# A graph attention layer on one core: the source one-hot is compared with node numbers kept in PSUM, and the score lives in PSUM

## Chip, cores and metric

The kernel runs on one core of a Trainium2 chip. The metric is the device time of one execution in microseconds, the median over several runs; lower is better.

## What is computed

A graph of 6250 nodes with 64 features each and 206250 edges, sorted by destination. Edge features go through a linear layer, source and destination nodes through three, and each node sums the weighted messages of its edges:

```python
Qh = (x @ Wq.T + bq).reshape(n, H, D)          # H = 4 heads, D = 16
Kh = (x @ Wk.T + bk).reshape(n, H, D)
Vh = (x @ Wv.T + bv).reshape(n, H, D)
Ee = (edge_attr @ We.T + be).reshape(-1, H, D)
score = (Kh[src] * Qh[dst] * (1.0 / np.sqrt(D)) * Ee).sum(-1)
score = jnp.exp(jnp.clip(score, -5.0, 5.0))
msg = Vh[src] * score[..., None]
wV = jax.ops.segment_sum(msg, dst, num_segments=n)
out = layernorm(x + wV.reshape(n, H * D))
```

## The kernel before

It has three stages. The first (to about 53 us) computes the tables of K and V (kv_table) and of Q (q_table) in HBM and makes the constants. The middle stage (to about 1797 us) goes once over the edges. The last adds x and normalises.

The middle stage works on 202 groups of 8 tiles of 128 edges (the last group has 4 tiles), with four slots of buffers, so that slot = group mod 4. Each engine has its own instruction stream, the same for every group but for the slot's parity, and semaphores with running counts order them. There is no planner: the order on each engine is that of its `step` function.

K and V of an edge's source node come in two ways. Most tiles are fetched by GpSimd, one indirect DMA of 128 rows per tile (L258, "gather"): 6 tiles in a group of even number, 7 in one of odd number. The other tiles, 2 and 1, are fetched by TensorE, for groups 2 to 199, with a one-hot: the 6250 nodes are cut in V = 7 blocks of 896 nodes, and a node's place in its block is p * U + u, with p the partition and U = 7 values of u. VectorE makes src_onehot (L784) with 128 x 896 elements, by comparing r_row (each edge's place in its block, a row spread over all partitions) with node_of (the numbers p * U + u, each repeated 128 times). TensorE multiplies it with x, split in two parts x_hi and x_lo, 14 matmuls of 448 columns into one of two xg_banks (L652, L653, `gather_x`). Of the 7 blocks VectorE keeps the right one (L795 x_sel and L801 xg_sb, `select_x`), and TensorE transposes it (L663) and projects it to K and V (L670), which ACT copies to kv (L756).

A step of VectorE for group g: kq = K times Q (L820, waits for the gathers and for L756), the sums of group g - 1 added to acc (L810, `add_sums`), kqe (L826), score (L829, a sum over D), score_c (L833, the clip), then for an even g a src_onehot of group g + 2 and for an odd g a select_x of group g + 1, then msg (L840, waits for ACT's exponential, L746, into p_ps), select_x of group g + 2, and src_onehot of group g + 3. Three src_onehot are made for two groups.

A step of TensorE for group g: the edges' linear layer of g + 1 (L615, L618), Q of g + 1 (L631), gather_x for g + 2, transposes for g + 1, the sums of messages of g (L641, waits for msg), the projection for g + 1, and for an even g a second gather_x for g + 2.

GpSimd issues the gathers of group g once its indices are loaded and msg of group g - 4 has been made, so it may run up to four groups ahead. SyncE loads all else.

PSUM has eight banks of 128 x 512 words. The two xg_banks are used in columns 0 to 447 of 512. Bank sum_ps holds two sums of messages (in 64 partitions), p_ps in columns 256 to 287, and is free beyond. src_onehot, r_row and node_of lie in SBUF, and so do score and score_c.

Of the kernel before, what the change touches and what calls it, by code (L numbers as in the profile page):

```python
# [5 lines left out]
F32 = mybir.dt.float32  # L6
F32R = mybir.dt.float32r
BF16 = mybir.dt.bfloat16
I32 = mybir.dt.int32
ALU = mybir.AluOpType  # L10
# [4 lines left out]
P = 128  # L15
N = 6250
E = 206250
F = 64
H = 4
# [5 lines left out]
T = 8  # L25
# [15 lines left out]
U = 7  # L41
V = 7
# [14 lines left out]
def gnn_kernel(nc, xT, x_blocks, w_kvq, We_t, be_row, src_tab, src_rows, src_cols, dst_tab,  # L57
               dst_rows, dst_first, attr, out):
    ctx = ExitStack()
    with ctx:  # L60
        def sb(name, shape, dt, stack=ctx):
            return stack.enter_context(nc.sbuf_tensor(name, shape, dt))

        def ps(name, shape, dt):
            return ctx.enter_context(nc.psum_tensor(name, shape, dt))

        def sem(name):
            return ctx.enter_context(nc.semaphore(name))
# [11 lines left out]
        src_block = sb("src_block", [P, Q], F32)  # L80
        minus_row = sb("minus_row", [P, G], F32)
        iota_v = sb("iota_v", [P, F * V], F32)
        node_of = sb("node_of", [P, U, P], F32)
        xg_t_sb = sb("xg_t_sb", [P, 2, P], F32)
        dst_neg = sb("dst_neg", [P, G, T], F32)
        base_i = sb("base_i", [P, G], I32)
# [14 lines left out]
        first = ExitStack()  # L101
# [16 lines left out]
        one_pass = sb("one_pass", [P, 1], F32, first)  # L118
        iota_i = sb("iota_i", [P, W], I32, first)
        iota_v_i = sb("iota_v_i", [P, F * V], I32, first)  # L120
        node_of_i = sb("node_of_i", [P, U, P], I32, first)
        row_i = sb("row_i", [P, 1], I32, first)
        row_f = sb("row_f", [P, 1], F32, first)
        x_nat = sb("x_nat", [P, U, F * V], F32, first)
# [9 lines left out]
        xg_banks = [ps(f"xg_bank{i}", [P, 4, P], F32) for i in range(2)]  # L134
        turn_bank = ps("turn_bank", [P, 4, P], F32)
        sum_ps = ps("sum_ps", [P, 4, P], F32)
        p_ps = sum_ps[:, 2, 0:T * H]
        kv_banks = [ee_ps[0], ee_ps[1], qe_ps[0], qe_ps[1]]
        q_banks = [turn_bank, sum_ps, xg_banks[0]]

# [19 lines left out]
        constants_made = sem("constants_made")  # L160
# [8 lines left out]
        iota_set = sem("iota_set")  # L169
# [52 lines left out]
        src_onehot_made = sem("src_onehot_made")  # L222
# [22 lines left out]
        def first_q(i, j):  # L245

            return (i + j // SLOTS) * PE_EACH + PE_BEFORE[j % SLOTS] - PE_SKIPPED
# [7 lines left out]
        def gather(pool, g, slot, first=0, end=T):  # L255

            for t in range(first, min(end, pool_tiles(g, slot))):
                pool.indirect_dma_start(  # L258
                    out=kv[:, slot, t, :], out_offset=None, in_=kv_table,
                    in_offset=bass.IndirectOffsetOnAxis(ap=idx[:, slot, t:t + 1], axis=0))\  # L260
                    .then_inc(kv_gathered[slot], 16)


        with nc.Block() as block:
# [37 lines left out]
            @block.gpsimd  # L302
            def _(pool):
                for c in range(DVE_ONES, CHUNKS):
                    pool.memset(xT_sb[F:P, c * CH * P:(c + 1) * CH * P], 1.0).then_inc(ones_set[1], 1)

                pool.wait_ge(ones_set[1], CHUNKS - DVE_ONES)
                pool.memset(we_sb[:, :], 0.0).then_inc(consts_zeroed, 1)
                pool.memset(be_sb[:, :, :], 0.0).then_inc(consts_zeroed, 1)
                pool.memset(q_win[:, :, :, :, :], 0.0).then_inc(consts_zeroed, 1)  # L310
                pool.memset(ones[:, :], 1.0).then_inc(consts_zeroed, 1)
                pool.memset(ident[:, :], 0.0).then_inc(ident_zeroed, 1)
                pool.wait_ge(ident_zeroed, 1)
                pool.affine_select(out=ident[:, :], in_=ident[:, :], compare_op=ALU.not_equal, fill=1.0,
                                   base=0, pattern=[[-1, P]], channel_multiplier=1).then_inc(ident_set, 1)
                pool.memset(xg_t_sb[:, :, :], 1.0).then_inc(consts_zeroed, 1)
                pool.iota(iota_i[:, :], pattern=[[1, W]], base=0, channel_multiplier=0).then_inc(iota_set, 1)
                pool.iota(iota_v_i[:, :], pattern=[[0, F], [1, V]], base=0, channel_multiplier=0).then_inc(iota_set, 1)
                pool.iota(node_of_i[:, :, :], pattern=[[1, U], [0, P]], base=0, channel_multiplier=U).then_inc(iota_set, 1)
                pool.wait_ge(iota_set, 3)  # L320
                pool.iota(row_i[0:W, :], pattern=[[0, 1]], base=0, channel_multiplier=1).then_inc(iota_set, 1)
                pool.iota(row_i[W:2 * W, :], pattern=[[0, 1]], base=0, channel_multiplier=1).then_inc(iota_set, 1)
                pool.wait_ge(iota_set, 5)

                pool.wait_ge(be_loaded, 16)
                pool.tensor_copy(be_parts[:, 0, :], be_f[:, :]).then_inc(be_step, 1)
                pool.wait_ge(be_step, 1)
                pool.tensor_tensor(be_rest[:, :], be_f[:, :], be_parts[:, 0, :], ALU.subtract).then_inc(be_step, 1)
                pool.wait_ge(be_step, 2)
                pool.tensor_copy(be_parts[:, 1, :], be_rest[:, :]).then_inc(be_step, 1)  # L330
                pool.wait_ge(be_step, 3)
                pool.tensor_tensor(be_parts[:, 2, :], be_rest[:, :], be_parts[:, 1, :], ALU.subtract).then_inc(be_step, 1)
                pool.wait_ge(be_step, 4)
                for part in range(3):
                    row = slice(32 * part, 32 * part + 1)
                    pool.tensor_copy(be_sb[row, :, :], be_parts[row, part:part + 1, :].to_broadcast([1, T, F]))\
                        .then_inc(be_step, 1)
                    pool.wait_ge(be_step, 5 + part)
                pool.wait_ge(idx_first, 16 * SLOTS)
                pool.wait_ge(kv_stored, 16 * CHUNKS)  # L340
                gather(pool, 0, 0, 0, EARLY[0])
                pool.wait_ge(limits_set, 4)
                pool.partition_all_reduce(limits_all[:, :], limits[:, :], P,
                                          bass.bass_isa.ReduceOp.max).then_inc(limits_joined, 1)
                for g in range(1, len(EARLY)):
                    gather(pool, g, g, 0, EARLY[g])
# [61 lines left out]
            def _(dve):  # L408
# [38 lines left out]
                check_destinations(5)  # L447
                dve.wait_ge(iota_set, 5)
                dve.tensor_copy(iota_w[:, :], iota_i[:, :]).then_inc(dst_step, 1)
                dve.tensor_copy(node_of[:, :, :], node_of_i[:, :, :]).then_inc(constants_made, 1)  # L450
                dve.tensor_copy(row_f[:, :], row_i[:, :]).then_inc(constants_made, 1)

                dve.wait_ge(src_loaded, 32)
# [14 lines left out]
                def third_part(c):  # L468
                    dve.wait_ge(q_part1, c + 1)
                    dve.tensor_tensor(q_stage[:, c * CH:(c + 1) * CH, 2, :], q_rest[:, c % 2, :, :],  # L470
                                      q_stage[:, c * CH:(c + 1) * CH, 1, :], ALU.subtract).then_inc(q_staged, 1)

                for c in range(CHUNKS):
# [6 lines left out]
                    if c >= 1:  # L480
                        third_part(c - 1)
                third_part(CHUNKS - 1)

                dve.wait_ge(x_split[0], 1)
                dve.tensor_tensor(x_lo[:, :, :], x_nat[:, :, :], x_hi[:, :, :], ALU.subtract).then_inc(x_split[1], 1)
                dve.wait_ge(limits_joined, 1)
# [12 lines left out]
                dve.tensor_scalar(base_i[:, :], base_f[:, :], one_pass[:, :], None, ALU.mult).then_inc(dst_step, 1)  # L499
                dve.scalar_tensor_tensor(out=dst_neg[:, :, :], in0=base_b, scalar=minus_general[:, :],  # L500
                                         in1=dst_neg[:, :, :], op0=ALU.mult, op1=ALU.add).then_inc(dst_step, 1)
                dve.wait_ge(constants_made, 3)
                dve.wait_ge(dst_step, 9)
                dve.tensor_scalar(minus_row[:, :], base_i[:, :], -1.0, row_f[:, :], ALU.mult, ALU.subtract)\
                   .then_inc(dst_step, 1)
# [8 lines left out]
        middle = ExitStack()  # L514
# [9 lines left out]
        xg_sb = sb("xg_sb", [P, 2, 2, F], F32, middle)  # L524
        kq = sb("kq", [P, T, F], F32, middle)
        kqe = sb("kqe", [P, T, F], F32, middle)
        score = sb("score", [P, T * H], F32, middle)
        score_c = sb("score_c", [P, T * H], F32, middle)
        msg = sb("msg", [P, 2, T, F], F32, middle)

        with nc.Fori(0, passes) as this_pass:
            with nc.Block() as block:
# [242 lines left out]
                def _(dve):  # L775
                    def make_src_onehot(g, i, j, k):

                        q, slot = first_q(i, j) + k, j % SLOTS
                        parity = (PE_BEFORE[slot] - PE_SKIPPED + k) % 2
                        if k == 0:  # L780
                            dve.wait_ge(r_loaded[slot], 16 * (i + j // SLOTS + (1 if slot >= PE_FROM else 0)))
                        if not (isinstance(q, int) and q < 2):
                            dve.wait_ge(x_gathered, q - 1)
                        dve.tensor_tensor(src_onehot[:, parity, :, :],  # L784
                                          r_row[:, slot, k:k + 1, :].to_broadcast([P, U, P]),
                                          node_of[:, :, :], ALU.is_equal).then_inc(src_onehot_made, 1)

                    def select_x(g, i, j, k):

# [23 lines left out]
                    def step(g, i, j):  # L813
# [21 lines left out]
                        if pe_tiles(g + 2, (j + 2) % SLOTS) == 2:  # L835
                            make_src_onehot(g + 2, i, j + 2, 1)
# [10 lines left out]
                        if pe_tiles(g + 3, (j + 3) % SLOTS):  # L847
                            make_src_onehot(g + 3, i, j + 3, 0)

                    make_src_onehot(PE_FROM, 0, PE_FROM, 0)  # L850
                    for g in range(SLOTS):
                        step(g, 0, g)
# [180 lines left out]
```

## Time and profile before

| | |
|---|---|
| median of 3 runs | 1816.32 us (1814.88 to 1819.0) |
| span of the profiled execution, first to last instruction | 1816.0 us |
| TensorE matmul busy | 1671.1 us (92%) |
| TensorE weight load busy (beside matmul) | 1483.1 us (82%) |
| VectorE busy | 1320.3 us (73%) |
| ScalarE (ACT) busy | 968.4 us (53%) |
| GpSimd busy | 1366.6 us (75%) |
| mean granted TensorE clock | 0.976 |

The profiled execution's time is known by its span; the runs' times stand at most 3 us from it. Busy time of an engine leaves out its waits and also the time in which it issues; engines work side by side, so the shares add up to more than one. L12 is line 12 of the kernel; PE is TensorE, PEld its weight load, DVE is VectorE, ACT is ScalarE, POOL is GpSimd. Idle time is given with what ended it; "issue" is idle time in which nothing is seen that was waited for.

### The profile page before, as it was taken

Reading aid. Unit: us, or ns where it says so; the run is one execution under the profiler, and the core shown is the slowest. Engines: PE = TensorE matmul, PEld = TensorE weight load, DVE = VectorE, ACT = ScalarE, POOL = GpSimd, SP = SyncE. Lnnn points to the kernel's source line nnn. Section 1 sums busy time; section 2 is a strip of 40 time slices with the busy share of each in tenths; the row PEclk is TensorE's granted clock in tenths of the full one; section 3 lists DMA queues with packets and bytes.
Section 4 is the critical chain, followed back from the end, with each engine's and each line's share of the span. In section 5 each row is a group of like instructions: output and inputs, shape, how many; then the busy total and the mean of one; then the engine's idle time right before and its main releaser. Section 6 shows DMA issues by size and latency. Waiting matters only on the chain. (4 is left out here: it accounts for less than half of the span.)

```text
span 1816.0 us, 47296 instructions
## 1 busy us (share of the span) xinstructions
PE 1671.1 (92%) x13047; PEld 1483.1 (82%) x13047; DVE 1320.3 (73%) x2197; ACT 968.4 (53%) x2864; POOL 1366.6 (75%) x1348
## 2 busy tenths in 40 slices
PE   6399999999999999999999999999999999999994
PEld 6388888888888888888888888888888888888883
DVE  6377777777777777777777777777777777777774
ACT  5355555555555555555555555555555555555553
POOL 5677777777777777777777777777777777777774
PEclk8699999999999999999999999999999999999995
DMA  7455444444444444444444444444444444444441
GB/s 234 129 139 136 127 132 126 127 126 129 130 123 124 134 129 124 128 133 127 128 133 127 122 132 130 125 125 135 127 124 125 133 129 125 123 128 132 127 114 61
DMA packets 198830, 234.44 MB, mean 129 GB/s; under 512 B 96742, under 2 KB 123180, under 8 KB 198684
## 3 DMA queue, kind: packets, MB, share of 16 engines
q1 hardware_dynamic: 156732, 147.96, 27.7%
q0 software_dynamic: 42080, 86.26, 19.5%
q8 instruction: 8, 0.13, 0.0%
q14 instruction: 10, 0.08, 0.0%
HBM read 226.67 MB, written 7.38 MB: 129 GB/s over the span
## 5 line engine op out<-in xcount | busy, mean ns | idle before, releaser
L258 POOL DMA_INDIRECT kv<-kv_table,idx x1315 | 1348.7, 1026 | 416.4 <-issue 402.2
L652 PE MATMUL xg_bank<-x_hi,src_onehot 128*128 128x448 f32 x2079 | 786.5, 378 | 6.7 <-DVE src_onehot L784 6.7
L653 PE MATMUL xg_bank<-x_lo,src_onehot 128*128 128x448 f32 x2079 | 759.7, 365 | 0.0
L723 ACT ACTIVATE distance<-iota_w,dst_neg 128x64 f32<-128x64 f32 x1612 | 428.4, 339 | 0.0
L652 PEld LDWEIGHTS xg_bank<-x_hi,src_onehot 128*128 128x128 f32 x2079 | 391.8, 188 | 35.3 <-DVE src_onehot L784 6.9
L653 PEld LDWEIGHTS xg_bank<-x_lo,src_onehot 128*128 128x128 f32 x2079 | 392.3, 189 | 27.3
L820 DVE TENSOR_TENSOR kq<-kv,qe_ps 128x512 f32<-128x512 f32 x202 | 138.5, 686 | 332.3 <-DMA kv<-kv_table,idx 325.6
L784 DVE TENSOR_TENSOR src_onehot<-r_row,node_of 128x896 fp32r<-128x896 f32 x297 | 322.9, 1087 | 25.0 <-DMA r_row<-r_table 25.0
L641 PE MATMUL sum_ps<-onehot,msg 128*64 128x64 f32 x3224 | 228.4, 225 | 77.6 <-DVE msg L840 77.6
L641 PEld LDWEIGHTS sum_ps<-onehot,msg 128*64 128x64 f32 x3224 | 208.8, 139 | 102.9 <-DVE msg L840 100.9
L749 ACT COPY xg_t_sb<-turn_bank 64x256 f32<-64x256 f32 x198 | 61.9, 312 | 330.6 <-PE turn_bank L663 240.8
L795 DVE SCALAR_TENSOR_TENSOR x_sel<-iota_v,src_block,xg_bank 128x448 f32<-128x448 f32 x297 | 201.1, 677 | 44.0 <-PE xg_bank L653 36.3
L618 PEld LDWEIGHTS ee_ps<-we_sb,attr_sb 128*128 128x128 f32 x1612 | 215.0, 194 | 6.5
L618 PE MATMUL ee_ps<-we_sb,attr_sb 128*128 128x128 f32 x1612 | 214.7, 277 | 0.0
L746 ACT ACTIVATE sum_ps<-score_c 128x32 f32<-128x32 f32 x202 | 40.5, 201 | 317.8 <-DVE score_c L833 317.7
L801 DVE TENSOR_REDUCE xg_sb<-x_sel 128x64 f32<-128x448 f32 x297 | 184.2, 620 | 10.2
L631 PE MATMUL qe_ps<-q_win,onehot_t 128*128 128x128 bf16 x2418 | 169.5, 220 | 2.2 <-DMA q_win<-q_table 1.6
L631 PEld LDWEIGHTS qe_ps<-q_win,onehot_t 128*128 128x128 bf16 x2418 | 153.7, 99 | 5.1 <-DMA q_win<-q_table 2.7
L709 ACT ACTIVATE dst_square<-dst_row,minus_row 128x512 f32<-128x512 int32 x202 | 143.6, 711 | 20.1 <-DMA dst_row<-dst_rows 20.1
L829 DVE TENSOR_REDUCE score<-kqe 128x32 f32<-128x512 f32 x202 | 138.3, 685 | 6.9
L840 DVE TENSOR_TENSOR msg<-kv,sum_ps 128x512 f32<-128x512 f32 x202 | 136.7, 677 | 1.1 <-ACT sum_ps L746 1.1
L826 DVE TENSOR_TENSOR kqe<-kq,ee_ps 128x512 f32<-128x512 f32 x202 | 136.3, 675 | 1.1 <-issue 0.3
(116 smaller groups left out, 1049.4 us busy)
## 6 DMA issues: line engine op xcount, KB each, us to landing
attr_sb<-attr SPq DMA_DIRECT2D x201, 256.0 KB
dst_row<-dst_rows SPq DMA_DIRECT2D x402, 128.0 KB
kv<-kv_table,idx POOLq DMA_INDIRECT x1315
r_row<-r_table SPq DMA_DIRECT2D x99, 128.0 KB, 3.1
q_win<-q_table SPq DMA_DIRECT2D x404, 24.0 KB
r_row<-r_table SPq DMA_DIRECT2D x99, 64.0 KB, 2.9
idx<-src_tab SPq DMA_DIRECT2D x206, 4.0 KB, 4.1
kv_table<-kv_stage SPq DMA_DIRECT2D x7, 448.0 KB, 3.8
```

What stands on the lines that cost most here:

```text
L258: pool.indirect_dma_start(out=kv[:, slot, t, :], out_offset=None, in_=kv_table, in_offset=bass.IndirectOffsetOnAxis(ap=idx[:, slot, t:t + ...
L618: mm = pe.matmul(ee[:, k * P:(k + 1) * P], attr_sb[:, slot, k * P:(k + 1) * P], we_sb[:, :], start=False, stop=(k == n - 1))
L631: mm = pe.matmul(bank(qe_ps[slot % 2], n * P)[:, k * P:(k + 1) * P], onehot_t[:, slot % 2, k * P:(k + 1) * P], q_win[:, slot, :, s, :], st ...
L641: mm = pe.matmul(sum_ps[0:F, slot % 2, 0:W], msg[:, slot % 2, t, :], onehot[:, slot, t, :], start=(t == 0), stop=(t == n - 1))
L652: pe.matmul(xg, src_onehot[:, parity, u, :], x_hi[:, u, :], start=(u == 0), stop=False)
L653: mm = pe.matmul(xg, src_onehot[:, parity, u, :], x_lo[:, u, :], start=False, stop=(u == U - 1))
L709: act.activation(dst_square[:, 0:n], dst_row[:, slot, 0:n], ACT.Square, bias=minus_row[:, ds(g, 1)]).then_inc(dst_squared, 1)
L723: made = act.activation(distance[:, t, :], iota_w[:, :], ACT.Square, bias=dst_neg[:, ds(g, 1), t:t + 1].rearrange("p o t -> p (o t)"))
L784: dve.tensor_tensor(src_onehot[:, parity, :, :], r_row[:, slot, k:k + 1, :].to_broadcast([P, U, P]), node_of[:, :, :], ALU.is_equal).then_ ...
L795: dve.scalar_tensor_tensor(out=x_sel[:, :, :].rearrange("p f v -> p (f v)"), in0=iota_v[:, :], scalar=src_block[:, ds(q, 1)], in1=bank(xg_ ...
L801: dve.tensor_reduce(xg_sb[:, j % 2, k, :], x_sel[:, :, :], AX_X, ALU.add).then_inc(x_summed, 1)
L820: dve.tensor_tensor(kq[:, 0:n, :], kv[:, slot, 0:n, 0:F], qe_ps[slot % 2][:, 0:n, :], ALU.mult).then_inc(kq_made, 1)
```

## The change

node_of is no longer a table of 128 x 896 words in SBUF. Its seven numbers for each partition are copied into columns 448 to 454 of both xg_banks, and L784 reads those of the bank of its parity, each number 128 times by a step of zero. The iota that makes them has 7 columns instead of 896. The cast in the setup goes, and two copies of seven columns are made later in the setup, after the last use of xg_banks[0] for Q. score and score_c move to columns 288 to 319 and 320 to 351 of bank sum_ps, so that L829 writes PSUM, L833 reads and writes it, and L746 reads it. No wait in the loop changes.

```diff
-        node_of = sb("node_of", [P, U, P], F32)
...
-        node_of_i = sb("node_of_i", [P, U, P], I32, first)
+        node_of_i = sb("node_of_i", [P, U], I32, first)
...
         p_ps = sum_ps[:, 2, 0:T * H]
+        score = sum_ps[:, 2, T * H:2 * T * H]
+        score_c = sum_ps[:, 2, 2 * T * H:3 * T * H]
+        node_of = [b[:, 3, F * V - 3 * P:F * V - 3 * P + U] for b in xg_banks]
...
-                pool.iota(node_of_i[:, :, :], pattern=[[1, U], [0, P]], base=0, channel_multiplier=U).then_inc(iota_set, 1)
+                pool.iota(node_of_i[:, :], pattern=[[1, U]], base=0, channel_multiplier=U).then_inc(iota_set, 1)
...
-                dve.tensor_copy(node_of[:, :, :], node_of_i[:, :, :]).then_inc(constants_made, 1)
...
+                for parity in range(2):
+                    dve.tensor_copy(node_of[parity], node_of_i[:, :]).then_inc(constants_made, 1)
+
                 dve.wait_ge(x_split[0], 1)
...
-                dve.wait_ge(constants_made, 3)
+                dve.wait_ge(constants_made, 4)
...
-        score = sb("score", [P, T * H], F32, middle)
-        score_c = sb("score_c", [P, T * H], F32, middle)
...
                         dve.tensor_tensor(src_onehot[:, parity, :, :],
                                           r_row[:, slot, k:k + 1, :].to_broadcast([P, U, P]),
-                                          node_of[:, :, :], ALU.is_equal).then_inc(src_onehot_made, 1)
+                                          node_of[parity].unsqueeze(2).to_broadcast([P, U, P]),
+                                          ALU.is_equal).then_inc(src_onehot_made, 1)
```

## Rows read from the trace of the kernel before

**Rows 1.** Part 1 of the page: busy time, share of the span, instructions.
```profile
PE 1671.1 (92%) x13047; PEld 1483.1 (82%) x13047; DVE 1320.3 (73%) x2197; ACT 968.4 (53%) x2864; POOL 1366.6 (75%) x1348
```

**Rows 2.** Groups by line: busy us, mean ns | idle us before, and its releasers.
```profile
L258 POOL DMA_INDIRECT kv<-kv_table,idx x1315 | 1348.7, 1026 | 416.4 <-issue 402.2 <-DVE msg L840 8.2 <-DMA kv_table<-kv_stage 6.0
...
L784 DVE TENSOR_TENSOR src_onehot<-r_row,node_of 128x896 fp32r<-128x896 f32 x297 | 322.9, 1087 | 25.0 <-DMA r_row<-r_table 25.0
...
L795 DVE SCALAR_TENSOR_TENSOR x_sel<-iota_v,src_block,xg_bank 128x448 f32<-128x448 f32 x297 | 201.1, 677 | 44.0 <-PE xg_bank L653 36.3
...
L801 DVE TENSOR_REDUCE xg_sb<-x_sel 128x64 f32<-128x448 f32 x297 | 184.2, 620 | 10.2
...
L820 DVE TENSOR_TENSOR kq<-kv,qe_ps 128x512 f32<-128x512 f32 x202 | 138.5, 686 | 332.3 <-DMA kv<-kv_table,idx 325.6 <-ACT kv L756 3.6 <-PE qe_ps L631 2.8
...
L840 DVE TENSOR_TENSOR msg<-kv,sum_ps 128x512 f32<-128x512 f32 x202 | 136.7, 677 | 1.1 <-ACT sum_ps L746 1.1
...
L833 DVE TENSOR_SCALAR score_c<-score 128x32 f32<-128x32 f32 x202 | 38.0, 188 | 7.0
```

**Rows 3.** GpSimd in order of time, the end of the gathers: start, duration in us.
```profile
1771.01 0.94 POOL L258 DMA_INDIRECT kv<-kv_table,idx  x1 [0.30 <-issue]
...
1789.74 0.94 POOL L258 DMA_INDIRECT kv<-kv_table,idx  x1 [0.30 <-issue]
```

**Rows 4.** Busy time of each engine in two stretches, clock, DMA share.
```profile
core 0: us, PE busy (x) PEld busy (x) DVE busy (x) ACT busy (x) POOL busy (x), PEclk, DMA share, GB/s
200.00:330.00 130.00, 130.00 (x1032) 116.26 (x1031) 100.80 (x166) 74.58 (x226) 100.42 (x98) 1.00 0.48 127
340.00:1790.00 1450.00, 1364.16 (x10684) 1205.12 (x10682) 1063.62 (x1757) 777.99 (x2345) 1116.26 (x1096) 0.99 0.47 127
```

**Rows 5.** GpSimd and VectorE in order of time: stretched gathers and one L784.
```profile
100.81 1.43 POOL L258 DMA_INDIRECT kv<-kv_table,idx  x1 [0.30 <-issue]
...
903.04 1.08 DVE L784 TENSOR_TENSOR src_onehot<-r_row,node_of 128x896 fp32r<-128x896 f32 x1
903.24 1.70 POOL L258 DMA_INDIRECT kv<-kv_table,idx  x1 [0.30 <-issue]
...
1756.93 1.29 POOL L258 DMA_INDIRECT kv<-kv_table,idx  x1 [0.30 <-issue]
```

**Rows 6.** What VectorE waited for, 200 to 330 us: total us, times, longest.
```profile
DVE x_sel L795 <- PE xg_bank L653: 18.6, 8, 2.5
DVE kq L820 <- DMA kv<-kv_table,idx: 3.1, 2, 2.4
```

**Rows 7.** VectorE in order of time: kq of groups 4, 24, 40 and 190.
```profile
111.01 0.69 DVE L820 TENSOR_TENSOR kq<-kv,qe_ps 128x512 f32<-128x512 f32 x1 [0.33 <-ACT kv L756]
...
272.39 0.69 DVE L820 TENSOR_TENSOR kq<-kv,qe_ps 128x512 f32<-128x512 f32 x1 [0.21 <-ACT kv L756]
...
405.89 0.69 DVE L820 TENSOR_TENSOR kq<-kv,qe_ps 128x512 f32<-128x512 f32 x1 [1.05 <-DMA kv<-kv_table,idx]
...
1699.68 0.69 DVE L820 TENSOR_TENSOR kq<-kv,qe_ps 128x512 f32<-128x512 f32 x1 [1.13 <-DMA kv<-kv_table,idx]
```

**Rows 8.** GpSimd in order of time: first and last gather of group 4.
```profile
83.47 0.94 POOL L258 DMA_INDIRECT kv<-kv_table,idx  x1 [6.38 <-DVE msg L840]
...
90.63 0.94 POOL L258 DMA_INDIRECT kv<-kv_table,idx  x1 [0.31 <-issue]
```

**Rows 9.** VectorE in order of time: kq of groups 199 to 201, one msg.
```profile
1777.18 0.69 DVE L820 TENSOR_TENSOR kq<-kv,qe_ps 128x512 f32<-128x512 f32 x1 [5.10 <-DMA kv<-kv_table,idx]
...
1780.01 0.69 DVE L840 TENSOR_TENSOR msg<-kv,sum_ps 128x512 f32<-128x512 f32 x1 [0.27 <-ACT sum_ps L746]
1787.16 0.69 DVE L820 TENSOR_TENSOR kq<-kv,qe_ps 128x512 f32<-128x512 f32 x1 [6.46 <-DMA kv<-kv_table,idx]
...
1792.78 0.42 DVE L820 TENSOR_TENSOR kq<-kv,qe_ps 128x256 f32<-128x256 f32 x1 [1.84 <-DMA kv<-kv_table,idx]
```

**Rows 10.** VectorE in order of time: setup, the wait ahead of x_lo.
```profile
46.10 3.42 DVE L485 TENSOR_TENSOR x_lo<-x_nat,x_hi 128x3136 fp32r<-128x3136 f32 x1 [2.08 <-ACT x_hi L403]
```

## The prediction

> **What bounds the kernel now.** I read the page first. TensorE is busy for 92% of the span and GpSimd for 75% [rows 1], which points at TensorE. But the GpSimd row counts only the bodies of the gathers: the group of L258 has 1315 gathers of 1026 ns on the mean, and the idle time before them is 402.2 us of "issue", that is of nothing that it waited for. On the other side stands VectorE, whose kq of each group sat idle for 325.6 us in all until gathered rows had landed [rows 2]. So GpSimd issues without a stop, and the others wait for what it fetches.
>
> The next view is GpSimd's order of time. Left alone, a gather takes 0.94 us and the next starts 1.2487 us after it: 15 steps from 1771.01 to 1789.74 [rows 3]. That beat is shorter than the 1.326 us of the middle of the run (98 gathers in 130 us, [rows 4]). The difference is stretched gathers, and they have one companion. At 903.24 a gather starts 0.20 us after the source one-hot of L784 began, and takes 1.70 us: 0.76 more, and it ends 0.82 us after L784's end at 904.12, as if most of it only began then [rows 5]. I went through all 1265 gathers that start between 100 and 1780 us. 223 last longer than 0.97 us (the first at 100.81, the last at 1756.93, [rows 5]), and every one of the 223 starts while an L784 is running; no other gather is stretched. Their excess over 0.942 us sums to 101.1 us. L784 is the only instruction in the loop that reads two large tiles from SBUF. 432 gathers began during L820, L826, L840 or L795, which read one tile from SBUF and the other from PSUM, and none was stretched; nor were those begun during the reductions, which read one.
>
> The last view is a comparison of two stretches. Over 200 to 330 us TensorE is busy 130.00 of 130.00 us, and VectorE waits for gathered rows only 3.1 us; over 340 to 1790 us TensorE has 85.8 us idle of 1450 [rows 4, 6]. The first is bound by TensorE, the second by the gathers. Their paces can be read from kq: group 4 at 111.01 and group 24 at 272.39 make 16.14 us for two groups; group 40 at 405.89 and group 190 at 1699.68 make 17.25 [rows 7]. Two groups need 13 gathers (6 and 7, since TensorE fetches 2 and 1 of the tiles), and 17.25 / 13 is 1.327: the stretched beat again. The kernel begins in the first regime because GpSimd has a lead there: the last gather of group 4 starts at 90.63 and kq of group 4 at 111.01 [rows 7, 8]. The lead shrinks by 1.1 us in two groups and is used up near 310 to 335 us.
>
> **The change part by part.** *L784 compares with PSUM.* It keeps its 297 runs and 896 columns, but only r_row comes from SBUF. By the 432 unstretched gathers it then holds up no gather. GpSimd's path from group 4 on: its first gather starts at 83.47 (held by msg of group 0, which doesn't change), its last at 1789.74 [rows 3, 8]. That is 1285 steps in 1706.27 us; at 1.2487 each they are 1604.6, so 101.7 us less, which agrees with the 101.1 summed above. What follows the last gather is fixed: kq of group 201 starts at 1792.78 [rows 9] and the span ends at 1816.0. By this path alone the span is 1816.0 - 101.7 = 1714.3.
>
> Here a rule of the Trainium skill speaks against the change. The row is the 1.70 us gather above [rows 5]. The page "SBUF — State Buffer", section "Who interferes with whom", says that GpSimd blocks against a VectorE instruction with two SBUF inputs only where it reads SBUF itself, and infers that a tensor_tensor leaves the generation of DMA descriptors alone, since that needs only the write side. By that inference there would be nothing to win and the sum would be 0 instead of 101.7. The trace disagrees for these gathers, which also read their indices from SBUF; the same section's first half fits it.
>
> *L784's own time.* Rows of equal width differ by source only a little: 128x448 takes 620 ns as the reduction L801 from SBUF and 677 as L795, which reads a PSUM bank; L840 reads its second input from PSUM with a step of zero, as the new L784 does, and takes 677 for 512 columns against 686 of L820 [rows 2]. So the bounds for L784 are its 1087 ns and 57 more. I take 1087. The upper bound is 0.17 us for two groups (3 one-hots), beside which VectorE has 29.2 us idle in 130, or 3.6 us for two groups, even in the stretch at TensorE's pace [rows 4]. That idle time hides it; without that cover it would cost 101 x 0.17 = 17 us.
>
> *TensorE's path.* This is what is late next. The gathers' new beat is 13 x 1.2487 = 16.23 us for two groups, and TensorE's pace 16.14. GpSimd starts with its lead of 111.01 - 91.57 = 19.4 us, of which some 2 are landing time, and now loses only 0.09 us in two groups, 9 us in the whole loop. So the lead never runs out, and TensorE sets the pace almost to the end. Group 198 is 97 pairs after group 4: its kq starts at 111.01 + 97 x 16.14 = 1676.6. Groups 198 to 201 have nothing left for TensorE to fetch but one tile of 199, and a step there is short: in the tail kq to the end of msg is 3.5 us (1777.18 to 1780.70, [rows 9]), and with the sums, the projection and its copy about 4.5. That puts kq of 199, 200 and 201 at 1681, 1685 and 1689 by the engines' own work. GpSimd, which still has 7, 8 and 4 gathers to do, allows them at 1777.18, 1787.16 and 1792.78 less 101.7: 1675.5, 1685.5 and 1691.1 [rows 9]. The gathers come last by about 2 us, and the end stays at 1714.3. So the two limits nearly meet, and nothing beyond the stretch is won.
>
> *Bank order.* The new L784 reads the bank that TensorE fills for the same parity. Its wait for x_gathered and TensorE's wait for src_onehot_made were there before; no wait is added. The same holds for score and score_c in the bank of the sums: VectorE writes score only after add_sums, which has waited for sums_made.
>
> *Score and clip in PSUM.* No row shows VectorE writing PSUM. L829 and L833 keep their widths, and L833 has 188 ns [rows 2]; by the 57 ns that at most separated a read of PSUM from one of SBUF, I bound the two together at nothing and 0.1 us more, and take nothing. They are under the idle time named above, and only the four tail groups would show it, 0.4 us. No gather is stretched by L833 alone, so nothing is won there.
>
> *Setup.* The cast of 128x896 goes; it can't have cost more than L784 at the same width, 1.1 us. Two copies of 7 columns come, each about as long as L833 (0.19 us, [rows 2]), placed ahead of L485, where VectorE idles 2.08 us for ACT's x_hi [rows 10]: they go into that wait, and cost 0.4 us without it. The smaller iota lies on GpSimd ahead of the 6.0 us for which its first gather waits for kv_table [rows 2]. Bounds: from 1.1 us won to 0.4 lost; I take 0.
>
> **Sum.** 1816.0 - 101.7 = 1714.3 for the span. A run's time stands 0.3 us above it (median 1816.32), and GpSimd, now closer behind msg in the first groups, may wait there up to 1 us more. Forecast: 1715 us, 5.6% faster. Its own range is 1707 to 1722.
>
> **Rivals.** *TensorE takes over at a worse pace.* For it: the slack at the end is only 2 us, 16.14 was read over ten pairs, and with longer one-hots or with TensorE never idle the pace might slip. Against it: the 130 us without idle time at a granted clock of 1.00, the 2.4 GHz level [rows 4]. Each 0.1 us in two groups adds 9.7 us once the 2 are gone; at 16.3 the time is 1714 + 16 - 2, about 1728.
>
> *Nothing changes,* as it would if the hold came from what L784 writes, or from its reading r_row, and not from the pair of inputs (the inference of the Trainium skill's page cited above would give the same time). Against it: L795 and L840 also read SBUF and write SBUF, without one stretched gather. Time 1816. A partial hold would lie between.
>
> *Slower: reading seven numbers 128 times each from PSUM is slow.* If L784 took twice its time, 2.17 us, VectorE's own chain for two groups would go from about 14.2 (2 x 3.5 of kq to msg with gaps, 3 x 2.4 of one-hot, select and reduce) to 17.5, above both 17.25 and 16.14: 85 pairs at 0.25 and 13 at 1.4 more, some 39 us, 1855. It decides from about 1 us more for one instruction. Against it is the 677 ns of L840, whose second input is just such a read.
>
> **Chances.** Forecast 0.78; TensorE at a worse pace (1722 to 1745) 0.12; nothing or a part (above 1745, to 1816) 0.06, 0.03 of it without a change; slower 0.03; faster than 1707 0.01. From 1707 to 1740 I leave out about 0.13. A difference under 0.2% (3.6 us) can't be told from none. Faster: 0.94; within 0.2%: 0.03; slower: 0.03.
>
> **What the profile after would show.** L258's mean falls from 1026 to about 946 ns, with no gather over 0.97 us in the loop. L784 stays near 1087 ns. kq's wait for gathered rows shrinks from 325.6 us to under 30, mostly in the last groups, and x_sel's wait for TensorE (18.6 us in the early 130 us, [rows 6]) grows to over 150. kq goes at 16.14 us for two groups from start to end, and TensorE's busy share is 97% or more. The prediction is wrong if stretched gathers remain (the hold isn't the pair of inputs), if L784 is well above 1.14 us, or if TensorE's pace exceeds 16.2.

## The result and the profile after

The changed kernel takes 1715.97 us (median of 4 runs, 1715.64 to 1717.27) against 1815.88 for the kernel before beside it: a ratio of 0.9453, interval 0.9436 to 0.9471, which is 5.5% faster. The profiled execution's span is 1713.8 us.

The page of the changed kernel answers to [rows 1]:

```profile
PE 1649.7 (96%) x13047; PEld 1479.4 (86%) x13047; DVE 1318.6 (77%) x2198; ACT 960.6 (56%) x2864; POOL 1263.1 (74%) x1348
```

GpSimd lost 103 us of busy time; VectorE kept its own within 2 us and ACT within 8. TensorE's fell by 21 us for the same 13047 instructions: its records are 10 us shorter in sum and overlap by 11 us more, and no work went from it. Work shrank only for the gathers. The groups by line answer to [rows 2]:

```profile
L260 POOL DMA_INDIRECT kv<-kv_table,idx x1315 | 1246.1, 948 | 416.5 <-issue 388.1
...
L798 DVE SCALAR_TENSOR_TENSOR x_sel<-iota_v,src_block,xg_bank 128x448 f32<-128x448 f32 x297 | 202.0, 680 | 248.5 <-PE xg_bank L655 240.7
L786 DVE TENSOR_TENSOR src_onehot<-r_row,xg_bank 128x896 fp32r<-128x896 f32 x297 | 320.0, 1078 | 24.8 <-DMA r_row<-r_table 24.8
...
L823 DVE TENSOR_TENSOR kq<-kv,qe_ps 128x512 f32<-128x512 f32 x202 | 137.9, 683 | 28.5 <-ACT kv L758 23.5
```

The mean gather went from 1026 to 948 ns. kq no longer waits for gathered rows (325.6 us before), and VectorE's waiting has moved to x_sel, which waits for TensorE. That is how a change of bound looks: the same idle time, with another releaser. In order of time, GpSimd and then VectorE near the place of [rows 5]:

```profile
905.73 0.94 POOL L260 DMA_INDIRECT kv<-kv_table,idx  x1 [0.30 <-DVE msg L843]
906.98 0.94 POOL L260 DMA_INDIRECT kv<-kv_table,idx  x1 [0.30 <-issue]
908.23 0.95 POOL L260 DMA_INDIRECT kv<-kv_table,idx  x1 [0.31 <-issue]
```

```profile
906.83 1.08 DVE L786 TENSOR_TENSOR src_onehot<-r_row,xg_bank 128x896 fp32r<-128x896 f32 x1
```

The gather of 906.98 begins 0.15 us into a one-hot and takes 0.94 us; before, one that began at 0.20 took 1.70. Of all gathers from 100 us to the end, 253 began during an L786, and none of them, and none of the others, is longer than 0.97 us. Before, 252 gathers had begun during an L784 (100 to 1780 us), and 223 of them were stretched. The windows answer to [rows 4], and three kq, of groups 4, 40 and 190, to [rows 7]:

```profile
200.00:330.00 130.00, 130.00 (x1035) 116.43 (x1034) 102.65 (x171) 73.98 (x226) 98.17 (x104) 1.00 0.51 136
340.00:1690.00 1350.00, 1343.58 (x10684) 1202.31 (x10683) 1062.05 (x1756) 770.23 (x2344) 1019.35 (x1080) 1.00 0.51 135
```

```profile
110.24 0.69 DVE L823 TENSOR_TENSOR kq<-kv,qe_ps 128x512 f32<-128x512 f32 x1 [0.33 <-ACT kv L758]
...
400.81 0.69 DVE L823 TENSOR_TENSOR kq<-kv,qe_ps 128x512 f32<-128x512 f32 x1 [0.22 <-ACT kv L758]
...
1611.83 0.69 DVE L823 TENSOR_TENSOR kq<-kv,qe_ps 128x512 f32<-128x512 f32 x1 [0.29 <-ACT kv L758]
```

TensorE is busy for 99.5% of the long stretch (340 to 1690 us), where it was for 94% (340 to 1790), and the 150 groups from 40 to 190 go at 16.15 us for two, the pace that the kernel before had only in its first 300 us. The kernel ends with the rows that answer to [rows 9], kq of groups 199 to 201:

```profile
1682.19 0.69 DVE L823 TENSOR_TENSOR kq<-kv,qe_ps 128x512 f32<-128x512 f32 x1 [2.01 <-ACT kv L758]
...
1685.64 0.68 DVE L823 TENSOR_TENSOR kq<-kv,qe_ps 128x512 f32<-128x512 f32 x1
...
1690.42 0.42 DVE L823 TENSOR_TENSOR kq<-kv,qe_ps 128x256 f32<-128x256 f32 x1 [0.37 <-DMA kv<-kv_table,idx]
```

### The profile page after: what moved, and what is told of

Read it like the earlier page. It is cut to its first block and busy times, and to the rows that moved or that the text cites. A ratio compares the mean times of both kernels' runs of the same rounds, so it can differ in the third digit from the quotient of the medians.

```text
span 1713.8 us, 47297 instructions
## 1 busy us (share of the span) xinstructions
PE 1649.7 (96%) x13047; PEld 1479.4 (86%) x13047; DVE 1318.6 (77%) x2198; ACT 960.6 (56%) x2864; POOL 1263.1 (74%) x1348
## 5 line engine op out<-in xcount | busy, mean ns | idle before, releaser
L260 POOL DMA_INDIRECT kv<-kv_table,idx x1315 | 1246.1, 948 | 416.5 <-issue 388.1
L798 DVE SCALAR_TENSOR_TENSOR x_sel<-iota_v,src_block,xg_bank 128x448 f32<-128x448 f32 x297 | 202.0, 680 | 248.5 <-PE xg_bank L655 240.7
L786 DVE TENSOR_TENSOR src_onehot<-r_row,xg_bank 128x896 fp32r<-128x896 f32 x297 | 320.0, 1078 | 24.8 <-DMA r_row<-r_table 24.8
L643 PE MATMUL sum_ps<-onehot,msg 128*64 128x64 f32 x3224 | 224.4, 223 | 8.6 <-DVE msg L843 8.6
L832 DVE TENSOR_REDUCE sum_ps<-kqe 128x32 f32<-128x512 f32 x202 | 140.0, 693 | 6.9
L829 DVE TENSOR_TENSOR kqe<-kq,ee_ps 128x512 f32<-128x512 f32 x202 | 135.4, 670 | 0.3 <-issue 0.3
L736 ACT ACTIVATE onehot<-distance 128x512 f32<-128x512 f32 x202 | 127.5, 631 | 10.4
```

Source lines behind the costliest of these rows:

```text
L260: pool.indirect_dma_start(out=kv[:, slot, t, :], out_offset=None, in_=kv_table, in_offset=bass.IndirectOffsetOnAxis(ap=idx[:, slot, t:t + ...
L643: mm = pe.matmul(sum_ps[0:F, slot % 2, 0:W], msg[:, slot % 2, t, :], onehot[:, slot, t, :], start=(t == 0), stop=(t == n - 1))
L786: dve.tensor_tensor(src_onehot[:, parity, :, :], r_row[:, slot, k:k + 1, :].to_broadcast([P, U, P]), node_of[parity].unsqueeze(2).to_broad ...
L798: dve.scalar_tensor_tensor(out=x_sel[:, :, :].rearrange("p f v -> p (f v)"), in0=iota_v[:, :], scalar=src_block[:, ds(q, 1)], in1=bank(xg_ ...
L832: dve.tensor_reduce(score[:, 0:n * H], kqe[:, 0:n, :].rearrange("p t (h d) -> p (t h) d", d=D), AX_X, ALU.add).then_inc(score_summed, 1)
```

## Experiments

Two things were open: what in the old one-hot held the gathers, and whether the new time really is one where two limits meet. The runs fell on chips in two conditions. On the first two chips the kernel before itself took 2749.65 and 2664.51 us instead of 1816. It has no trace there, but in the traces of the kernels beside it TensorE issued with gaps. A piece of the weight loads, in order of time, from the kernel of the first experiment:

```profile
1035.34 0.19 PEld L654 LDWEIGHTS xg_bank<-x_hi,src_onehot 128*128 128x128 f32 x1 [0.55 <-issue]
1036.07 0.19 PEld L655 LDWEIGHTS xg_bank<-x_lo,src_onehot 128*128 128x128 f32 x1 [0.55 <-issue]
1036.79 0.19 PEld L654 LDWEIGHTS xg_bank<-x_hi,src_onehot 128*128 128x128 f32 x1 [0.53 <-issue]
1037.51 0.28 PEld L655 LDWEIGHTS xg_bank<-x_lo,src_onehot 128*128 128x128 f32 x1 [0.54 <-issue]
1038.92 0.29 PEld L654 LDWEIGHTS xg_bank<-x_hi,src_onehot 128*128 128x128 f32 x1 [1.13 <-issue]
```

One load each 0.72 us or twice that, where 0.20 is usual, and nothing that it waits for. From 100 us on this kernel has 777 steps between weight loads of more than 0.6 us, 965 us in all; the changed kernel on the chip of the result has none. On such a chip the length of the gathers can still be read, but the time says nothing of them, because GpSimd isn't the bound. So each run is read for what its chip can show.

**One half of the change at a time.** The first kernel takes the one-hot's part alone:

```diff
-        score = sum_ps[:, 2, T * H:2 * T * H]
-        score_c = sum_ps[:, 2, 2 * T * H:3 * T * H]
...
+        score = sb("score", [P, T * H], F32, middle)
+        score_c = sb("score_c", [P, T * H], F32, middle)
```

> The source one-hot compares with PSUM as in the change, score and score_c stay in SBUF. Main theory (only the one-hot held GpSimd's gathers): the time of the changed kernel, 1716 us, no gather over 0.97 us. Rival (the fp32 clip from SBUF to SBUF holds gathers too): some of the 101 us comes back, stretched gathers begin during the clip; each could cost at most its 0.19 us, 202 x 0.19 = 38 us, so up to 1754.

> The one-hot alone in PSUM, score and score_c in SBUF, once more. Main theory: no stretched gather (mean 948 ns); where TensorE issues without gaps 1716 us against 1816 us of the kernel before, where it has gaps (the kernel before at 2660 to 2750 us) the same time as the kernel before within 1.5%, because GpSimd then waits for msg and not for itself. Rival (score in PSUM carries a part of the 100 us): above 1720 us where TensorE has no gaps.

The second takes the score's part alone (the same lines the other way round, in the kernel before):

> Only score and score_c in PSUM, the one-hot compares with the SBUF table as before. Main theory: 1816 us, within 3 us, some 220 stretched gathers with 101 us of excess. Rival (the clip holds gathers): up to 38 us faster.

Where TensorE had gaps: one-hot alone 2757.59 us, ratio 1.0061 (1.0019 to 1.0103), mean gather 949 ns; score alone 2750.52 us, ratio 0.9974 (0.9926 to 1.0023), mean gather 989 ns. Groups by line, of the one and of the other:

```profile
L258 POOL DMA_INDIRECT kv<-kv_table,idx x1315 | 1247.7, 949 | 1441.9 <-DVE msg L843 1060.3 <-issue 376.1 <-DMA kv_table<-kv_stage 5.5
```

```profile
L260 POOL DMA_INDIRECT kv<-kv_table,idx x1315 | 1300.3, 989 | 1375.4 <-DVE msg L840 986.4 <-issue 382.2 <-DMA kv_table<-kv_stage 6.8
```

With the score alone the hold is there (40 ns x 1315 = 53 us of GpSimd's time: 172 stretched gathers, every one begun during the one-hot, so the rival that the clip holds gathers falls). It is worth nothing here, since GpSimd waits some 1000 us for msg anyway. The 0.6% by which the one-hot alone came out slower has no explanation here. On a chip without gaps the one-hot alone took 1717.55 us, ratio 0.9459 (0.9438 to 0.9481), with a mean gather of 950 ns. The two intervals, this one and that of the whole change, overlap nearly fully: the one-hot's part carries the gain, and the score's part carries none of it that can be seen. The score's part was not timed alone on a chip without gaps.

**Small source, still in SBUF.** It separates PSUM from the size of the table.

```diff
+        node_small = sb("node_small", [P, 2, U], F32)
...
-        node_of = [b[:, 3, F * V - 3 * P:F * V - 3 * P + U] for b in xg_banks]
+        node_of = [node_small[:, b, :] for b in range(2)]
```

> As the changed kernel, but the seven numbers lie in SBUF and are read from there with a step of zero. Main theory (two SBUF inputs hold GpSimd, whatever their size): 1816 us, some 220 stretched gathers. Rival (the hold comes from streaming a table of 896 words, a small or repeated source is harmless): 1716 us.

> The same kernel as the one with the seven numbers in SBUF, on another chip if TensorE issues there without gaps. In the first run on a chip where TensorE has gaps of 0.5 us and more between its instructions, the gathers were stretched again (989 ns on the mean against 949), and the time was that of the kernel before there. Main theory on a chip like the first: 1816 us and a mean of 1026 ns. Rival (a small source is harmless for the time): 1716 us.

Both chips had gaps: 2759.71 us, ratio 1.0039 (0.9994 to 1.0083), and 2680.07 us, ratio 1.001 (0.9966 to 1.0054). The mean gather was 989 and 991 ns; the group of the second:

```profile
L261 POOL DMA_INDIRECT kv<-kv_table,idx x1315 | 1303.2, 991 | 1323.7 <-DVE msg L844 932.5 <-issue 385.6 <-DMA kv_table<-kv_stage 5.7
```

Seven numbers in SBUF hold the gathers as the table did (989 in the run with the table on the same chip as the first). One one-hot of the second run and the gather that began 0.09 us into it:

```profile
293.93 1.08 DVE L787 TENSOR_TENSOR src_onehot<-r_row,node_small 128x896 fp32r<-128x896 f32 x1
294.02 1.80 POOL L261 DMA_INDIRECT kv<-kv_table,idx  x1 [0.30 <-issue]
```

The rival, that a small source is harmless, falls. What it would do to the time where GpSimd is the bound was not measured.

**Inputs swapped.** In every harmless instruction of the trace before, SBUF was the first input.

```diff
-                                          r_row[:, slot, k:k + 1, :].to_broadcast([P, U, P]),
                                           node_of[parity].unsqueeze(2).to_broadcast([P, U, P]),
+                                          r_row[:, slot, k:k + 1, :].to_broadcast([P, U, P]),
```

> As the changed kernel, with the two inputs of the comparison swapped: the PSUM numbers are the first input, the SBUF row the second. In every instruction that left gathers alone in the trace before, the SBUF tile was the first input. Main theory (it takes two SBUF inputs): 1716 us, no stretched gather. Rival (whatever is the second input and lies in SBUF holds GpSimd): about 1816 us and some 220 stretched gathers.

> The kernel with swapped inputs again. It had no stretched gather on the chip with the gaps (949 ns). Main theory on a chip like the first: 1716 us. Rival (the SBUF row as second input holds GpSimd): 1816 us.

Again gaps on both chips: 2747.11 us, ratio 0.9918 (0.9863 to 0.9972), and 2729.06 us, ratio 1.0148 (1.003 to 1.0266). The two contradict each other in sign, which shows how far such a chip's times can be trusted: not within 1.5%. The gathers are clear, 949 and 948 ns; the group of the second run:

```profile
L260 POOL DMA_INDIRECT kv<-kv_table,idx x1315 | 1246.1, 948 | 1409.1 <-DVE msg L843 1012.5 <-issue 389.4 <-DMA kv_table<-kv_stage 7.2
```

So it isn't the place of the SBUF input but that there are two of them.

**Part of the columns.** The comparison is split: 512 columns against SBUF, 384 against PSUM.

```diff
-                        dve.tensor_tensor(src_onehot[:, parity, :, :],
-                                          r_row[:, slot, k:k + 1, :].to_broadcast([P, U, P]),
-                                          node_of[parity].unsqueeze(2).to_broadcast([P, U, P]),
+                        dve.tensor_tensor(src_onehot[:, parity, 0:4, :],
+                                          r_row[:, slot, k:k + 1, :].to_broadcast([P, 4, P]),
+                                          node_small[:, 0:4].unsqueeze(2).to_broadcast([P, 4, P]),
+                                          ALU.is_equal)
+                        dve.tensor_tensor(src_onehot[:, parity, 4:U, :],
+                                          r_row[:, slot, k:k + 1, :].to_broadcast([P, U - 4, P]),
+                                          node_of[parity][:, 4:U].unsqueeze(2).to_broadcast([P, U - 4, P]),
                                           ALU.is_equal).then_inc(src_onehot_made, 1)
```

> The comparison in two instructions: the first 512 of 896 columns against numbers in SBUF, the other 384 against PSUM. Main theory (a gather is held until the reads of the instruction with two SBUF inputs end): the excess goes with the square of the instruction's length, since both the chance of a gather beginning in it and the mean rest of it shrink; (0.59/0.99) squared is 0.36, so 36 us of 101 come back, 1752 us. Rival (the cost goes with the columns): 4/7 of 101, 1774 us. Rival (any such instruction costs a fixed hold): 1816 us.

> The comparison in two instructions: 512 of 896 columns against numbers in SBUF, the other 384 against PSUM. The run on a chip with gaps had a mean gather of 957 ns, against 989 with all 896 columns in SBUF and 948 with none. Main theory (a gather is held until the reads of the instruction with two SBUF inputs end, so the excess goes with about the square of its length): 36 of 101 us come back, some 1752 us, mean gather 975 ns. Rival (the cost goes with the columns): 58 us, 1774 us. Rival (a fixed hold): 1816 us.

With gaps 2724.86 us, without an interval, and a mean gather of 957 ns (65 stretched gathers, 11.3 us). Without gaps 1727.37 us, ratio 0.9512 (0.9494 to 0.953): some 10 us above the changed kernel and below all three expectations. Three groups of the second run say why:

```profile
L261 POOL DMA_INDIRECT kv<-kv_table,idx x1315 | 1254.5, 954 | 416.5 <-issue 399.7 <-DVE msg L849 11.4 <-DMA kv_table<-kv_stage 5.5
...
L788 DVE TENSOR_TENSOR src_onehot<-r_row,node_small 128x512 fp32r<-128x512 f32 x297 | 204.2, 687 | 25.1 <-DMA r_row<-r_table 25.1
...
L829 DVE TENSOR_TENSOR kq<-kv,qe_ps 128x512 f32<-128x512 f32 x202 | 138.0, 683 | 20.0 <-ACT kv L760 12.6 <-issue 1.6
```

The mean gather is 954 ns, not 975. From 100 us on only 14 gathers are stretched, by 4.5 us in all, where the square law gave 36. The hold itself is as that law has it. A gather and its one-hot:

```profile
906.45 0.68 DVE L788 TENSOR_TENSOR src_onehot<-r_row,node_small 128x512 fp32r<-128x512 f32 x1
906.49 1.46 POOL L261 DMA_INDIRECT kv<-kv_table,idx  x1 [0.30 <-issue]
```

The gather ends 0.82 us after the one-hot does, as the one of 903.24 did in the kernel before. So do all the others: the six traces with stretched gathers have 808 of them, and each ends 0.81 to 0.84 us after the end of the instruction with two SBUF inputs in which it began. A gather that is left alone takes 0.94, so it seems that about its first 0.125 us run freely and the rest waits (an estimate: 0.942 less the 0.817 that most of the 808 need afterwards). It loses what is left of that instruction less 0.125 us, and next to nothing if it begins in its last 0.16 us.

What failed is how often they met. The law takes every offset of a gather in the one-hot as equally likely. For the kernel before that comes out at 292 x (1.087 - 0.125)^2 / (2 x 1.2487) = 108 us, where 101 were measured, and for this one at 37. Here two groups take 16.26 us and 13 gathers at this run's beat of 1.251 take 16.26 as well, so the offsets hardly move from one pair of groups to the next: of the 120 gathers that began during an L788, 90 did so in its last 0.16 us. The 14 hits come in four bunches, at 110 to 117, 549 to 572, 906 to 913 and 1297 to 1320 us. That the loss is so small is luck.

The 10 us are not the hold but TensorE's pace. No kq waits for gathered rows, and the last one starts at 1701.66, 6 us after the last gather's start at 1695.69, so that the 4.5 us of hold stay hidden. (1623.23 - 403.73) / 75 is 16.26 us for two groups from kq 40 to kq 190, 0.11 more than in the changed kernel, and 97 times 0.11 is 11 us:

```profile
403.73 0.69 DVE L829 TENSOR_TENSOR kq<-kv,qe_ps 128x512 f32<-128x512 f32 x1
...
1623.23 0.69 DVE L829 TENSOR_TENSOR kq<-kv,qe_ps 128x512 f32<-128x512 f32 x1 [0.15 <-ACT kv L760]
```

From start to start, the weight loads of the source fetch (L656, L657) take 0.07 us more of these 0.11 and those of the transposes 0.04. Why stays open; that 13 gathers also make 16.26 may be chance or a coupling. The times of all three theories in the expectation fell.

**Less work for TensorE.**

```diff
-                            pe.matmul(xg, src_onehot[:, parity, u, :], x_hi[:, u, :], start=(u == 0), stop=False)
-                            mm = pe.matmul(xg, src_onehot[:, parity, u, :], x_lo[:, u, :], start=False, stop=(u == U - 1))
+                            mm = pe.matmul(xg, src_onehot[:, parity, u, :], x_hi[:, u, :], start=(u == 0), stop=(u == U - 1))
```

> The changed kernel without the 7 of 14 matmuls of each source fetch that multiply with x_lo, so that x is fetched with less precision; TensorE loses 3 x 7 x 0.2 = 4.3 us of its 16.14 for two groups. Main theory (GpSimd's path of 1286 gathers at 1.2487 us ends with the kernel too, at most 2 us apart): 1714 us, the changed kernel's time within 4 us, and kq waits for gathered rows again for over 300 us. Rival (TensorE alone is the bound after the change): clearly faster, 100 x 4.3 us less down to VectorE's 14.2 us for two groups, some 1530 us.

> The changed kernel without the 7 of 14 matmuls of each source fetch that multiply with x_lo (x is fetched with less precision), so TensorE loses 3 x 7 x 0.2 = 4.3 us of its 16.14 for two groups. On a chip where TensorE issues without gaps. Main theory (GpSimd's path of 1285 steps of 1.2487 us ends within 2 us of TensorE's): 1714 us, no more than 4 us from the changed kernel, kq waiting for gathered rows again for over 200 us, at 16.23 us for two groups. Rival (TensorE alone is the bound after the change): some 1530 us.

With gaps 2631.3 us, ratio 0.984 (0.9767 to 0.9913): even there 2079 fewer matmuls bought little. Without gaps 1718.27 us, ratio 0.9464 (0.9446 to 0.9482). TensorE's busy time fell from 1649.7 to 1352.6 us and the kernel's time not at all: it is 2 us longer, as its gathers' beat of 1.2510 makes GpSimd's path 3 us longer than at 1.2487. The group of kq and one window:

```profile
L822 DVE TENSOR_TENSOR kq<-kv,qe_ps 128x512 f32<-128x512 f32 x202 | 138.7, 687 | 271.0 <-DMA kv<-kv_table,idx 246.2 <-ACT kv L757 18.3 <-PE qe_ps L633 5.7
```

```profile
340.00:1690.00 1350.00, 1084.72 (x8669) 940.76 (x8833) 1044.03 (x1733) 758.04 (x2314) 1020.72 (x1080) 0.92 0.51 134
```

kq waits for gathered rows again, 246.2 us, and none of the gathers is stretched: this is GpSimd's bare path. It runs from 82.61 to 1690.10, 1285 steps of 1.2510 us. Only in the first groups, where GpSimd still has its lead, does the rest show its own pace: kq of group 4 at 105.52 and of group 14 at 173.92 make 13.7 us for two groups, against 16.25 afterwards.

**Less work for GpSimd.** This kernel leaves out K and V of the first tile of each group, which are zeros there:

```diff
-            for t in range(first, min(end, pool_tiles(g, slot))):
+            for t in range(max(first, 1), min(end, pool_tiles(g, slot))):
```

(and the counts of `gathered` one lower for each group, with kv's first tiles set to zero once).

> The changed kernel without the first gather of every group (that tile's K and V are zeros, set once), so GpSimd has 11 instead of 13 gathers for two groups, 13.7 us. Main theory (TensorE's pace of 16.14 us for two groups sets the loop, GpSimd ends only some 2 us behind it): 1710 to 1716 us, kq still at 16.14 us for two groups, GpSimd waiting for msg for over 200 us. Rival (GpSimd still is the bound after the change and TensorE follows): 202 x 1.25 = 250 us less, down to VectorE's 14.2 us for two groups, some 1530 us.

1713.19 us, ratio 0.9432 (0.9415 to 0.9449), on the same chip as the last. What GpSimd waited for, in the whole span:

```profile
POOL kv L260 <- DVE msg L844: 303.5, 195, 8.0
POOL kv L260 <- issue: 285.5, 917, 4.2
```

202 gathers fewer are 252 us of GpSimd's time. It spends them waiting for msg, 303.5 us, and the kernel gains no more than 3 us (the intervals overlap), 5 against the kernel with less TensorE work. kq goes at (1611.31 - 400.01) / 75 = 16.15. Taken together: without 18% of TensorE's busy time the kernel takes 1718 us, without 15% of the gathers 1713, and with everything 1716. Neither engine alone can be relieved for more than some 3 us. Both relieved together were not run; the 13.7 us for two groups above hint at what the next limit would allow.

## Why the prediction was right

*What bounded the kernel.* Right: 101.6 us less on GpSimd's path gave 100 us less time, with TensorE's work unchanged, and the idle time moved from one releaser to the other. TensorE at 92% was not the bound, and GpSimd at 75% was.

*The hold.* The step "101.7 us less on GpSimd's path" is the whole of the sum. The path from group 4's first gather to the last is now 82.71 to 1687.38, 1604.7 us for the 1604.6 forecast. Its cause, two SBUF inputs in one VectorE instruction, was an inference from some 430 harmless gathers beside instructions that all had SBUF first. The runs with seven numbers in SBUF and with swapped inputs turned it into something shown. The rival that what L784 writes, or r_row, makes the hold fell with the result itself. The page "SBUF — State Buffer" of the Trainium skill, section "Who interferes with whom", infers that a tensor_tensor leaves descriptor generation alone. For these gathers it would have meant no stretch, and 223 were stretched. They also read their indices from SBUF, and that GpSimd is held where it reads SBUF itself fits; whether this read or the making of the descriptors is what waits, no run separates.

*L784's own time.* 1078 ns for 1087 forecast. The small loss of being delayed itself is gone: up to 1164 ns before, for one-hots that began within 0.05 us of a gather's start, and 1087 at most after. Seven numbers read 128 times each from PSUM cost nothing, and the slower rival falls.

*TensorE's path.* 16.15 us for two groups from 40 to 190 (16.14 forecast), group 198's kq at 1676.28 (1676.6), and the last three at 1682.19, 1685.64 and 1690.42 (1681, 1685.5 and 1691.1). The two limits met as worked out, and the last kq still waited 0.37 us for its gathers. That TensorE would take over at a worse pace fell for this kernel; the split comparison shows that such a thing exists and costs 10 us. x_sel's wait for TensorE grew to 240.7 us (over 150 forecast), and kq's for gathered rows fell to 0.4 us (under 30 forecast). TensorE's busy share is 96%, not 97% or more: the forecast took its busy time as unchanged, and it fell by 21 us.

*Score and clip.* L829 went from 685 to 693 ns and L833 from 188 to 199, the exponential from 201 to 181: nothing, as taken.

*Setup.* x_lo (now L489) starts at 45.46 instead of 46.10, after a wait of 1.94 us, and the first gather of group 4 at 82.71 instead of 83.47. The term was taken as 0 inside its bounds; it is about the 0.5 us by which the span came out under 1714.3.

*From span to time.* This small term was read wrongly. Each run's time stands 1.8 to 1.9 us above its own span (1715.64 against 1713.8 for the profiled one), not 0.3: the prediction set the span of one execution against the median of others, which differ by 4 us among themselves. With 1.8 the forecast span of 1714.3 would have given 1716.1. Beside the 100 us neither this nor the 0.5 us above matters.

## What to carry to other kernels

Add a DMA-issuing engine's gaps to its busy time before ruling it out: GpSimd at 75% was full, and the engine at 92% was waiting for it. Where gathers issued by GpSimd bound a kernel, look for those that last longer than their fellows and for what runs on VectorE when they start. Here an instruction with both inputs in SBUF held a gather that began in it until it was done, and a few columns left over in a PSUM bank were enough to free them. How much such a hold costs depends on how the two beats meet: 14 hits against 292 one-hots in one kernel, 223 in another. Before the next step, work out the path of the engine that comes next: here it lay within 2 us, so that the stall was all there was to win, and on chips where another engine was the bound the same stall was worth nothing.

## What the runs showed of the hardware

- On two of the chips TensorE's weight loads came one each 0.72 us (or 1.4) in bursts of up to 14, often about 60 loads apart in the stretch that was looked at (1000 to 1200 us), with no wait behind them in the trace, and the kernel before took 2665 and 2750 us instead of 1816. The mean granted clock was 0.83 there instead of 0.98. The other engines' durations were the same (L786 1079 ns, gathers 949). The cause isn't known.
- With 4.3 us less TensorE work for two groups its mean granted clock in the loop was 0.92 instead of 1.00, so that it spent part of the loop at the lower level, and the matmuls that were left still didn't set the time.
- Seven numbers in PSUM, each read 128 times, stream at the rate of a table in SBUF: 1078 to 1081 ns for 896 columns, in either input place, against 1082 to 1087 with two inputs in SBUF.
- A stretched gather ended 0.81 to 0.84 us after the end of the instruction with two SBUF inputs in which it began, in each of the 808 cases of a stretched one, whether 896 or 512 columns were compared. Not stretched were those that began in its last 0.16 us, and some that began in its first 0.1 us (13 of 24 in the kernel before).
